# Attention projections in three half-precision products instead of one in single precision, a third place for weight chunks, and new orders of work

## The reference

```python
x = L0_attn_hidden_states                                   # 4 x 512 x 512
x = _layernorm(x + _L0_attn_ref(x, Wq, Wk, Wv, Wo))         # 32 heads of 16, 8 key heads, RoPE, causal
x = _layernorm(x + _L0_ffn_ref(x, ...))                     # 4-bit weights, 512 -> 1376 -> 512, gated
x = _layernorm(x + _L1_attn_ref(x, ...))                    # 512 -> 128, two rounds of "hydra", 128 -> 512
x = _layernorm(x + _L1_ffn_ref(x, ...))                     # int weights, 512 -> 1792 -> 512, gated
# in _L0_attn_ref:
q, k, v = hidden_states @ Wq.T, hidden_states @ Wk.T, hidden_states @ Wv.T
# ... RoPE on q and k, causal softmax of q k / 4, times v ...
return out @ Wo.T
```

## Time and profile before

| | |
|---|---|
| device time, 3 runs | 1449.06, 1452.62, 1453.59 us (median 1452.62) |
| profiled execution | 1458.4 us, its span 1456.3 us, mean granted clock 0.977 |
| PE busy | 1377.5 us, 95% of the span |
| DVE, ACT, POOL busy | 1045.2, 789.0, 721.5 us (72, 54, 50%) |

### The profile page before, as it was taken

The page is one execution under the profiler, slowest core; times in us unless marked ns, Lnnn a source line. Parts: engine busy times, 40 slices in busy tenths (PEclk is TensorE's granted clock), DMA queues, the critical chain, the costliest instruction groups (busy, mean ns, idle before and its releaser), DMA issues.

```text
span 1456.3 us, 32199 instructions
## 1 busy us (share of the span) xinstructions
PE 1377.5 (95%) x11646; PEld 996.9 (68%) x11646; DVE 1045.2 (72%) x2322; ACT 789.0 (54%) x1737; POOL 721.5 (50%) x915
## 2 busy tenths in 40 slices
PE   6889999999999989999999889999999999999998
PEld 3546776776677668668777666676767767676875
DVE  5886987887886778776876958877686869575121
ACT  3886877777676667777876243433424432421211
POOL 3655655756567577686545434353425343341211
PEclk8779999999999999999999999999999999999999
DMA  8654478578876556785463100451001000100000
GB/s 251 151 125 95 110 152 158 124 140 151 183 135 129 127 138 138 157 163 99 112 142 77 44 1 16 181 185 49 9 1 45 15 1 8 37 16 16 1 15 16
DMA packets 245120, 135.04 MB, mean 93 GB/s; under 512 B 164506, under 2 KB 228226, under 8 KB 244066
## 3 DMA queue, kind: packets, MB, share of 16 engines
q1 hardware_dynamic: 243724, 132.91, 40.0%
q10 hardware_dynamic: 1238, 0.07, 0.1%
HBM read 75.00 MB, written 19.92 MB: 65 GB/s over the span
## 4 chain that ended last, share of the span: by engine, by line
PE 50%; DVE 19%; issue 7%; DMA 7%; POOL 7%; ACT 5%; SPq 4%; DVEq 0%; ACTq 0%; POOLq 0%
PE ps L1906 14%; PE ps L1731 7%; PE ps L1926 6%; PE ps L1803 3%; PE ps L1692 3%; DMA pt<-stp 2%; PE ps L1793 2%; PE ps L1718 2%; PE ps L1746 2%; DVE xraw L1504 2%; PE ps L1856 2%; PE ps L1819 2%; DMA vs<-in_s1u 2%; DVE nmax L1337 2%; DMA vs<-in_s1g 2%
## 5 line engine op out<-in xcount | busy, mean ns | idle before, releaser
L1906 PE MATMUL ps<-x3h,w1gu 128*128 128x256 f16 x1792 | 299.7, 273 | 5.2 <-DVE prod L1574 5.2
L1207 ACT ACTIVATE Pe<-ps,nmax 128x256 f32<-128x256 f32 (+3 forms) x512 | 251.6, 535 | 72.2 <-DVE nmax L1337 58.1
L1337 DVE TENSOR_REDUCE nmax<-ps 128x1 f32<-128x384 f32 (+3 forms) x352 | 220.6, 634 | 41.4 <-PE ps L1796 39.6
L1906 PE MATMUL ps<-x3l,w1gu 128*128 128x256 f16 x896 | 244.4, 273 | 0.0
L1906 PEld LDWEIGHTS ps<-x3h,w1gu 128*128 128x128 f16 x1792 | 175.5, 98 | 31.5 <-DVE prod L1574 8.2
L1332 DVE TENSOR_TENSOR pt<-ps,pt 128x512 f16<-128x512 f32 (+1 forms) x240 | 152.6, 636 | 33.5 <-ACT pt L1193 31.1
L1102 POOL TENSOR_TENSOR int1l<-prod,int1h 128x256 f16<-128x256 f32 x112 | 93.3, 836 | 147.9 <-ACT int1h L1293 147.9
L1193 ACT ACTIVATE pt<-ps 128x512 f16<-128x512 f32 (+1 forms) x240 | 134.9, 562 | 57.0 <-PE ps L1803 55.2
L1793 PE MATMUL ps<-kT,qT 128*128 128x256 f16 (+3 forms) x512 | 139.8, 307 | 9.6 <-ACT Pe L1207 8.6
L1803 PE MATMUL ps<-identf,Pe 128*128 128x128 f32 x880 | 142.0, 282 | 1.3 <-DVE pt L1332 1.2
L1819 PEld LDWEIGHTS ps<-V,pt 128*128 128x128 f16 x2560 | 97.8, 96 | 41.3 <-issue 17.1
(11 more groups left out here) (245 smaller groups left out, 3407.6 us busy)
## 6 DMA issues: line engine op xcount, KB each, us to landing
w1gu<-w_gu SPq DMA_DIRECT2D x7, 1024.0 KB, 8.3
x_dram<-xr SPq DMA_DIRECT2D x18, 256.0 KB, 3.2
xr<-in_x SPq DMA_DIRECT2D x16, 256.0 KB, 5.4
x2a<-x_dram SPq DMA_DIRECT2D x4, 1024.0 KB, 5.3
vq<-in_q1g SPq DMA_DIRECT2D x28, 128.0 KB, 2.4
vz<-in_z1g SPq DMA_DIRECT2D x28, 128.0 KB, 3.8
vs<-in_s1g SPq DMA_DIRECT2D x28, 128.0 KB, 4.4
w_gu<-vh SPq DMA_DIRECT2D x56, 64.0 KB, 2.2
```

The source lines that it names most:

```text
L1207: ins = act.activation(Pe[:, u % 2, x * w:(x + 1) * w], ps[:, u % 2, x * w:(x + 1) * w], ACT.Exp, bias=nmax[:, u % 4, x:x + 1])
L1337: dve.tensor_reduce(nmax[:, u % 4, 0:g], ps[:, u % 2, 0:g * w].rearrange("p (g w) -> p g w", g=g), AX, ALU.max, negate=True).then_inc(sem( ...
L1906: ins = pe.matmul(ps[:, bank, piece * H2:piece * H2 + H2], w1gu[:, j // 2, 2 * piece + pw, k, cols], px[:, k, h * H2:h * H2 + H2], start=( ...
```

## The change

1. From tile 2 on, `proj` multiplies an fp16 high part and an fp16 rest of x (`xte`, and a new DVE step `xtl`) by the same parts of the weights, in three products instead of one in fp32. Tiles 0 and 1 stay in fp32. The same holds for `wo` in all 16 tiles (new DVE step `atl`).
2. The fp32 weights land in `stp` and in three places of `xr`, and are split at the start: `wq_hi` and `wo_hi` on ACT, `wq_lo` and `wo_lo` on DVE. The loads of Wo, of the x of tiles 4 to 6, and the first DMA turn wait for that. Weights are scaled by 64, taken back in the RoPE tables, in `x1_sum` and in the column of ones of V.
3. `NPT` goes from 6 places to 5. Tile 12 leaves `PT_TILES`: its 16 DMA turns go to PE. Tile 7's `p_lo` goes from DVE to POOL.
4. W1's chunks have three places (`NVQ`), and their ranks lie 4 apart instead of 3.
5. The planner plans a consumer on another engine later than the producer's planned end (`MARGIN`), by 1.5 us behind `pt`, `w1c` and `x1_load`, 2 us behind `x_load` and 2.5 us behind `dq` and `dk`. `FFN0_AT` has new numbers. All orders follow from it.
6. Three pairs on POOL and DVE wait on the engine's own semaphore instead of on a named one.

```diff
-NPT, NST = 6, 3
-PT_TILES, PT_HEADS = (3, 6, 7, 12, 13, 14, 15), (0, 2)
-LO_POOL = (13, 14, 15)
+NPT, NST = 5, 3
+PT_TILES, PT_HEADS = (3, 6, 7, 13, 14, 15), (0, 2)
+LO_POOL = (7, 12, 13, 14, 15)
+NVQ = 3
+NF32 = 2
+WA_SCALE = 64.0
...
+MARGIN = {'pt': 1500, 'w1c': 1500, 'dq': 2500, 'dk': 2500, 'x_load': 2000, 'x1_load': 1500}
-CH1_AT = [CH0_AT[-1] + 6 + 3 * c for c in range(NC1)]
+CH1_AT = [CH0_AT[-1] + 6 + 4 * c for c in range(NC1)]
...
-FFN0_AT = [(99, 111), (115, 158), (158, 215), (230, 273), (334, 409), (394, 695), (647, 652), (366, 544)]
+FFN0_AT = [(831, 935), (508, 609), (583, 592), (336, 413), (398, 716), (656, 799), (359, 490), (535, 600)]
...
-            sp.dma_start(wqkv[:, :, :], A["wqkvT"].rearrange("(k p) n -> p k n", p=P)).then_inc(sem("ld_wqkv"), 16)
+            for n, to in enumerate((load_a, load_b)):
+                sp.dma_start(to.rearrange("p (k n) -> p k n", n=QKV), A["wqkvT"][2 * n * P:2 * n * P + 2 * P].rearrange("(k p) n -> p k n", p=P)).then_inc(sem("ld_wa"), 16)
...
+            if kind == "wq_lo":
+                dve.wait_ge(sem("wa_hi"), t + 1)
+                hi, lo = (wq[h][:, t, 0:512].rearrange("p (h v c) -> p h v c", v=2, c=HD) for h in (0, 1))
+                for v in range(2):
+                    dve.scalar_tensor_tensor(out=lo[:, :, v, :], in0=wq_load[t][:, 256 * v:256 * v + 256].rearrange("p (h c) -> p h c", c=HD),
+                                             scalar=WA_SCALE, in1=hi[:, :, v, :], op0=ALU.mult, op1=ALU.subtract)
+                dve.scalar_tensor_tensor(out=wq[1][:, t, 512:QKV], in0=wq_load[t][:, 512:QKV], scalar=WA_SCALE,
+                                         in1=wq[0][:, t, 512:QKV], op0=ALU.mult, op1=ALU.subtract).then_inc(sem("wa_lo"), 1)
...
+            if kind in ("xtl", "atl"):
+                to, source = (xT, "xT") if kind == "xtl" else (aT, "atr")
+                dve.wait_ge(sem("xte" if kind == "xtl" else "ate"), t + 1)
+                dve.tensor_tensor(to[:, 1, :, :].rearrange("p k n -> p (k n)"), ps[:, JOB_BANK[source, t], :],
+                                  to[:, 0, :, :].rearrange("p k n -> p (k n)"), ALU.subtract).then_inc(sem(kind), 1)
...
+                for at, (px, pw) in enumerate(((0, 0), (0, 1), (1, 0))):
+                    ins = pe.matmul(to, xT[:, px, k, :], wq[pw][:, k, cols], start=(k == 0 and at == 0), stop=(k == KD - 1 and at == 2))
...
-            ins = pe.matmul(ps[:, bank, :], aT[:, k, :], wo[:, k, :], start=(k == 0), stop=(k == KD - 1))
+            for at, (px, pw) in enumerate(((0, 0), (0, 1), (1, 0))):
+                ins = pe.matmul(ps[:, bank, :], aT[:, px, k, :], wo[pw][:, k, :], start=(k == 0 and at == 0), stop=(k == KD - 1 and at == 2))
```

More of the change, by code:

```diff
@@ L307, in way_in @@
         if NI <= t < RING:
-            A("SP", "x_load", t, 1200, [], r - 10)
+            A("SP", "x_load", t, 1200, [("wo_lo", KD - 1)] if t < NI + 3 else [], r - 10)
         if t == 0:
             A("SP", "wqkv_load", t, 6000, [], -100)
-            A("SP", "wo_load", t, 4000, [], 10)
+            for k in range(KD):
+                A("ACT", "wq_hi", k, 900, [("wqkv_load", 0)], -11 + 0.1 * k)
+                A("DVE", "wq_lo", k, 960, [("wq_hi", k)], -11 + 0.1 * k)
+            A("SP", "wo_load", t, 4000, [("wq_lo", KD - 1), ("proj", NF32 - 1, PROJ_PIECES - 1)], WO_AT)
+            for k in range(KD):
+                A("ACT", "wo_hi", k, 550, [("wo_load", 0)], WO_AT + 2, chain="wq_hi")
+                A("DVE", "wo_lo", k, 690, [("wo_hi", k)], WO_AT + 2, chain="wq_lo")
         if t >= RING:
@@ L314, in way_in @@
         A("PE", "xT", t, 440, [("x_load", t) if t >= NI else None, ("proj", t - 1, PROJ_PIECES - 1) if t else None], r, takes=1)
-        A("ACT", "xte", t, 620, [("xT", t), ("proj", t - 1, PROJ_PIECES - 1) if t else None], r, frees=("xT", t))
-        e = self.pieces("proj", t, PROJ_PIECES, 860, [("xte", t), ("wqkv_load", 0)], r, takes=2)
+        A("ACT", "xte", t, 620, [("xT", t), ("proj", t - 1, PROJ_PIECES - 1) if t else None], r, frees=("xT", t) if t < NF32 else None)
+        if t < NF32:
+            e = self.pieces("proj", t, PROJ_PIECES, 860, [("xte", t), ("wqkv_load", 0)], r, takes=2)
+        else:
+            A("DVE", "xtl", t, 690, [("xte", t)], r, frees=("xT", t))
+            e = self.pieces("proj", t, PROJ_PIECES, 640, [("xtl", t), ("wq_lo", KD - 1)], r, takes=2)
         A("DVE", "qk_c", t, 820, [e, ("q_lo", t - 1) if t else None, ("k_lo", t - 1) if t else None], r)
@@ L344, in attention @@
         if u in PT_DMA:
-            A("ACT", "p_hi", u, 170 + 0.8 * c, [("exp", u), ("pt", PT_DMA[m - NST]) if m >= NST else None], u)
+            A("ACT", "p_hi", u, 170 + 0.8 * c, [("exp", u), ("pt", PT_DMA[m - NST]) if m >= NST else ("wo_lo", KD - 1)], u)
             if t in LO_POOL:
@@ L364, in way_out @@
         A("PE", "atr", t, 440, [("attn", NOG * t + NOG - 1)], r, takes=1)
-        A("ACT", "ate", t, 610, [("atr", t), ("wo", t - 1, WO_PIECES - 1) if t else None], r, frees=("atr", t))
-        e = self.pieces("wo", t, WO_PIECES, 860, [("ate", t), ("wo_load", 0)], r)
+        A("ACT", "ate", t, 610, [("atr", t), ("wo", t - 1, WO_PIECES - 1) if t else None], r)
+        A("DVE", "atl", t, 690, [("ate", t)], r, frees=("atr", t))
+        e = self.pieces("wo", t, WO_PIECES, 640, [("atl", t), ("wo_lo", KD - 1)], r)
         A("DVE", "x1_sum", t, 690, [e], r, frees=("wo", t))
@@ L1232, in act_stream @@
                     act_gate(act, key)
-                if kind in ("xte", "st_hi", "etq0", "etk0", "ate", "fxh", "f0_hi", "y16"):
+                if kind in ("xte", "wq_hi", "wo_hi", "st_hi", "etq0", "etk0", "ate", "fxh", "f0_hi", "y16"):
                     act_job(act, kind, key)
@@ L1594, in dve_stream @@
                     dve_gate(dve, kind, key)
-                if kind in ("qk_c", "qk_s", "v", "etq1", "x1_sum", "bn1", "x1", "fxl", "bn2", "x2"):
+                if kind in ("wq_lo", "wo_lo", "xtl", "atl", "qk_c", "qk_s", "v", "etq1", "x1_sum", "bn1", "x1", "fxl", "bn2", "x2"):
                     dve_job(dve, own, kind, key)
@@ L1636, in bank_free @@
                     pe.wait_ge(sem("deq_w"), key + 1)
-                if kind == "xT":
+                if kind == "xT" and key < NF32:
                     pe.wait_ge(sem("xte"), key + 1)
+                if kind == "xT" and key >= NF32:
+                    pe.wait_ge(sem("xtl"), key - NF32 + 1)
                 if kind == "proj":
@@ L1645, in bank_free @@
                 if kind == "atr":
-                    pe.wait_ge(sem("ate"), key + 1)
+                    pe.wait_ge(sem("atl"), key + 1)
                 if kind == "wo":
```

140 lines of the change are left out of this document (89 added, 51 removed).

## The result

The changed kernel takes 1417.26 us (median of 4 runs, 1415.61 to 1419.78) against 1450.84 us (4 runs, 1446.26 to 1453.59) for the kernel before on the same chip: ratio 0.9763, 95% interval 0.974 to 0.9787. The forecast was 1429 us, the range 1411 to 1447. It is faster by 33.6 us where 24 were forecast.

A forecast was written before the change was run, and what follows sets the result against it. PE's amount of work was taken as the limit from about 100 us on. 1458.4 - 29.1 (products) + 7.7 (tile 12) + 4.5 (start) - 7 (waits) = 1434.5 us, less 5.8 to the median: 1429 us, range 1411 to 1447.

The forecast's parts named there:

- The products: `proj` and `wo` on PE: three fp16 products cost less than one in fp32, 31.6 us less in all.
- Tiles 2 and 3: Their products' saving of 2.5 us lies before the first feed-forward product, where PE waits for DVE, so counted as hidden.
- Tile 12: 16 units of three transposes come back to PE from DMA turns: 7.7 us more.
- The start: Table scalings and `wq_lo` go ahead of tile 0's `qk_c` on DVE: 4.5 us more, bounds 0 and +12.
- The bound of +12: Upper bound for the start: `wq_lo` and `wo_lo` run like the slowest subtraction in four or five cases, 4.5 + 4 x 1.9.
- The waits: Margins and W1's third place remove waits for turns and loads: 7 us less, bounds 0 and -20.
- the waits dissolve: Rival: margins and third place take -20 instead of -7, start costs 2 us less: 1414 or 1411 us; chance 0.10.
- No gain: Rival: the `score`, `nmax`, `exp` loop of a unit sets the pace, PE merely idles more: 1453 to 1457 us; chance 0.08.
- Five places: Rival: fewer `pt` places delay turns and `exp`; 0.18 us lost per unit gives 1464 us, slower than before; chance 0.08.
- The prediction's marks: Values expected in the profile after, such as PE busy near 1354 us, last `pv` near 763, turn waits below 8.

The follow-up runs named there:

- the four-product run: The changed kernel in its exact order, with a fourth product, low by low, added in every `proj` and `wo` product: 1440.95 us, ratio 0.9929.
- The run with later splits: The changed kernel with `wq_hi` and `wq_lo` moved behind the fourth chunk's unpacking and tile 0's `v`: 1414.03 us, ratio 0.977.
- margins and refitted ranks: The kernel before with three fp16 products and their splits, the change's `MARGIN`, and `FFN0_AT` fitted to that: 1428.21 us, ratio 0.9849.
- the products alone: The changed kernel with places, tiles, W1 ranks, margins and `FFN0_AT` set back, only the three fp16 products, splits and loads remaining: 1455.56 us, ratio 1.0032.
- old ranks: The changed kernel with only `FFN0_AT`, the ranks of the first feed-forward block's eight halves, set back to the numbers of before: 1447.7 us, ratio 0.9989.

## Why the prediction was right, and where it was not

The sign and the range held, and the mechanism in its main step: with the order held, most of a us of products saved is a us of time. What the prediction did not have is that this holds only for orders fitted to the new durations. It took these orders as given; that they were fitted is what kept the gain. In the profiles the last `pv` came 41 us earlier where I had 23; some 8 us of the difference are the profiled executions.

By its sum, PE's work before the last `pv` was to fall by 23.0 us (-31.6, +0.9 for the last tile's `wo`, +7.7) and its idle time to stay (-7, +4.5 and the hidden 2.5). The idle time did stay (-1.3 us), but by terms that were each off: 11.1 us more in the start and 12.3 us less in the body. The work fell by 40.0. From each record's start to the next one's, the products account for 37.9 us of this, the transposes for +3.8, and instructions that the change left alone for 5.9, part of it the granted clock (last section). Point by point:

- **The products** (-31.6): the distances in fp16 were right. Twelve records of `wo` take 2.60 us after (112.53 to 115.13), the 2.59 of the working. Those in fp32 were short. Between 165 and 740 us, from start to start, `wo` went from 3.50 to 2.59 us per tile where the working had 3.45 and 2.59, and `proj` from 5.50 to 3.89 where it had 5.18 and 3.91. For all tiles that is 37.1 us instead of 31.6. The earlier trace rows show a few products in one unbroken piece; why fp32 products take more in their places is not shown. The busy times exaggerate it (`wo` 3.74 to 2.75, `proj` 6.13 to 4.42).
- **Tiles 2 and 3** (2.5 us counted as hidden): the four-product run speaks against it, since its start grew by 9.0 us.
- **Tile 12** (+7.7): the transposes' line rose by 4.5 us of busy time (142.0 to 146.5), all tiles together.
- **The start** (+4.5 on `qk_c`): 16.24 became 20.30, +4.1. Right in size. Still the first feed-forward product came 5.3 us earlier, where I had 160 to 168 us; 3.0 of the 5.3 are already in the plans (151.3 and 148.3 us). The run with later splits, with the first feed-forward product 2.5 us earlier still, says that about that much of the shift was on the path. The bound of +12 can be checked now. The `wq_lo` instructions ran at 0.42 us, with POOL without work beside them. Of the four `wo_lo`, the two that overlap a subtraction of two SBUF operands on POOL took longer:

```profile
61.14 1.24 DVE L1458 SCALAR_TENSOR_TENSOR wol<-stp,woh 128x512 f16<-128x512 f32 x1 [0.25 <-ACT woh L1182]
70.60 0.64 DVE L1458 SCALAR_TENSOR_TENSOR wol<-stp,woh 128x512 f16<-128x512 f32 x1
72.43 1.34 DVE L1458 SCALAR_TENSOR_TENSOR wol<-stp,woh 128x512 f16<-128x512 f32 x1
74.12 0.68 DVE L1458 SCALAR_TENSOR_TENSOR wol<-xr,woh 128x512 f16<-128x512 f32 x1
```

```profile
60.67 1.17 POOL L1041 TENSOR_TENSOR w0ul<-wv,w0uh 128x512 f16<-128x512 f32 x1 [1.40 <-ACT w0uh L1265]
...
71.46 1.76 POOL L1041 TENSOR_TENSOR w0gl<-wv,w0gh 128x352 f16<-128x352 f32 x2
```

Two times 0.6 us, not four times 1.9. The prediction quoted a rule for this, that the two engines contend for their SBUF interface when a VectorE instruction has two SBUF inputs (the Trainium skill, "GPSIMD Engine Reference", Specifications). The two long rows agree with it, and so does the last one, which has POOL idle beside it. The `wo_lo` at 70.60 runs beside a small product on POOL (`attn`, 70.76 to 71.50) and was not slowed; there POOL's instruction took 0.74 us, where its line has a mean of 0.41.

- **The waits** (-7): the body's idle time fell by 12.3 us, but PE's named waits for turns by only 3.0. The weak step is that I read the margins' worth from the named waits (6.8 us for turns). With margins and refitted ranks the idle time before the last `pv` fell by 8.1 us, where the waits for turns had been 4.8. A plan in which transfers land exactly as planned slips by 41 to 49 us here, one with 1.5 to 2.5 us of room behind each by 21 to 33. Of the 41.3 us, the plan accounts for 14.3 and the slip for 27.0, the difference of the profiled executions included. The rival "the waits dissolve" (1414 or 1411) was nearer to the 1417 measured than the forecast was, and had 0.10. That its number is near is in part luck: before the last `pv` there is hardly less idle time in all than before.
- **No gain** was given 0.08, on the argument that feed-forward products fill PE's gaps and "a saved us lets them move forward". For the products alone its time is what was measured (1455.6 us, where it had 1453 to 1457), and PE idles more. Its mechanism is shown in part only: the waits for `exp` are 12.3 us of the body instead of 4.9, those for turns 9.6 instead of 6.8. The argument against it fails at the last `pv`: the products that move ahead of it shorten the tail by little or nothing (old ranks: 11.8 us less work, no us less time), because the chain behind it then finds PE without other work. What the products save is only kept if the order leaves that filler behind and the idle time doesn't grow.
- **Five places**: no sign of this rival; PE's waits for `exp` are 7.8 us in all, and the change is faster with five places. No run changed the number of places alone.
- The prediction's marks: three held, the tail within 3 us of 670 (it is 670.3), the waits for turns below 8 (3.8 us, and 5.0 for the weight loads), the idle time before the last `pv` (53.9 against 55). The first feed-forward product, the last `pv` (744.5 against 763) and PE's busy time (1335 against 1354) missed on the good side. POOL's wait for loads missed (36.0, I had under 30), and DVE is at 82% up to the last `pv`, the upper edge.

What the runs leave open: how the last 11 us (1428.2 to 1417.3) divide between the third place, the five places and tile 12. The two kernels with margins and tile 12 on turns slip by 29.2 and 32.9, the four without by 21.4 to 26.0, which speaks for tile 12; but no run changed it with refitted ranks. The third place can't be taken away within the change's orders, because with two places they end in a circle of waits. Nor is it shown how much of the slip is due to turns, loads, or durations that the planner has wrong, or what fitted orders with margins would give in fp32.

## What to carry to other kernels

Where a planner or hand-set ranks order the work, the direct cost of an edit and its measured effect can differ by more than the whole gain, in both directions: compare variants only after the ranks are fitted to each, or with the order held fixed. Room behind transfers in the plan can be worth more than the waits that the profile names after them: kernels planned with it kept closer to their plans here, in every case. And before counting a saved microsecond on a full engine, ask which work moves into it, and whether the stretch that this work leaves gets any shorter.

## What the runs showed of the hardware

The same program can start at a different granted clock, and in the start it did not matter here. Two profiles of the same orders, 60 to 100 us, first that of the change, then that with all ranks moved by +10 (busy times as in the earlier trace rows, the clock is 0.83 and 0.70):

```profile
60.00:100.00 40.00, 29.29 (x218) 16.43 (x217) 37.07 (x68) 31.95 (x72) 24.25 (x25) 0.83 0.73 181
```

```profile
60.00:100.00 40.00, 32.41 (x218) 17.85 (x215) 36.33 (x67) 31.55 (x70) 24.14 (x25) 0.70 0.75 174
```

PE is busy for 3.1 us more at the lower clock, and up to the first feed-forward product for 6.0 us more (125.8 against 119.8), yet that product comes at 158.0 against 158.2 us and the last `pv` at 746.3 against 744.5. PE's idle time took up what the lower clock cost. So of the 16.4 us less on PE in the start (mean clock 0.90 against 0.85), a part is clock and no gain, which a comparison of busy times alone would have booked as one. This does not make the start free of PE's work: with four products instead of three PE is busy for 12.0 us more up to the first feed-forward product (131.8 against 119.8), and that product comes 9.0 us later.
